# Query blocks eight ahead of the attention units instead of nine, the mixes on POOL by quarters, and the last residuals in another order

## What is computed

```python
xn = layernorm(x)                                   # (8, 100, 1024)
kv = concat([ctx, xn], axis=1)                      # (8, 461, 1024)
q = rms_norm((xn @ Wq) per head, q_norm_w)          # 32 heads of 128
k = rms_norm((kv @ Wk) per head, k_norm_w)          # 8 key heads
v = (kv @ Wv) per head
probs = softmax(q k^T / sqrt(128))                  # 4 query heads share one key head
x1 = x + tanh(g_xattn) * ((probs @ v) as rows @ Wo)
# then, on y = layernorm(x1):
logits = y @ router_w.T + router_b; two best of 8 experts, gates normalised
x2 = x1 + tanh(g_ffn) * sum over the two experts of gate * ((y @ A_e^T) @ B_e^T) * 0.5
```

## Time and profile before

| | |
|---|---|
| median of three runs | 1689.81 us |
| the profiled execution | 1685.8 us, of which the span of instructions is 1684.0 us |
| PE busy | 1650.3 us (98% of the span) |
| DVE, ACT, POOL busy | 1176.9, 877.3, 889.1 us |
| TensorE clock granted over the span | 0.998 of full speed |
| units and query blocks | about 684 to 1436 us |
| output product and tail | about 1321 to 1684 us |

### The profile page before, as it was taken

One profiled execution on the slowest core, in us unless ns is written; L12 is line 12 of the kernel. 1 busy time (PEld: TensorE's weight loads), 2 busy tenths in 40 slices (PEclk: granted clock), 3 DMA queues, 4 the chain that ended last, 5 costly groups with the idle time before them and its releaser, 6 DMA issues.

```text
span 1684.0 us, 26179 instructions
## 1 busy us (share of the span) xinstructions
PE 1650.3 (98%) x9120; PEld 1470.7 (87%) x9120; DVE 1176.9 (70%) x2054; ACT 877.3 (52%) x1663; POOL 889.1 (53%) x700
## 2 busy tenths in 40 slices
PE   7999999999999999999999999999999999999997
PEld 6788888678888879999999999999999889999995
DVE  7788886677777752677677777776766777556676
ACT  5545554544544431566666666666666666443432
POOL 1344443134434420777777777777776455563131
PEclk9999999999999999999999999999999999999999
DMA  5567778736566647556666666655556566687551
GB/s 200 157 171 235 232 207 249 194 112 188 151 180 164 159 161 235 173 166 208 197 213 198 198 204 189 191 190 180 182 171 205 187 215 218 229 281 248 222 178 58
DMA packets 238503, 323.87 MB, mean 192 GB/s; under 512 B 53300, under 2 KB 193396, under 8 KB 233380
## 3 DMA queue, kind: packets, MB, share of 16 engines
q1 hardware_dynamic: 237796, 315.65, 60.3%
q10 hardware_dynamic: 576, 6.55, 1.0%
HBM read 212.18 MB, written 109.97 MB: 191 GB/s over the span
## 4 chain that ended last, share of the span: by engine, by line
PE 89%; DVE 6%; ACT 3%; issue 2%; DMA 0%; POOL 0%; DVEq 0%; SPq 0%; ACTq 0%; POOLq 0%
PE bank L991 26%; PE bank L993 25%; PE bank L992 25%; PE bank L1129 5%; PE bank L1096 2%; PE bank L1025 1%; PE bank L1335 1%; DVE wo_lo L2024 1%; DVE mx L2004 1%; DVE at_lo L2026 1%; ACT pr L1611 1%; ACT w_hi L1427 1%; PE bank L1346 0%; DMA wr<-Wkv 0%; DVE pT_lo L1998 0%
## 5 line engine op out<-in xcount | busy, mean ns | idle before, releaser
L911 POOL TENSOR_SCALAR pr<-pr,rr 100x461 f32<-100x461 f32 x256 | 371.1, 1457 | 162.1 <-DVE rr L2019 162.1
L991 PE MATMUL bank<-w_hi,a_hi 128*128 128x512 f32 (+1 forms) x856 | 341.2, 399 | 11.0 <-DVE a_lo L1794 8.5
L993 PE MATMUL bank<-w_hi,a_lo 128*128 128x512 f32 (+1 forms) x856 | 335.2, 392 | 0.0
L992 PE MATMUL bank<-w_lo,a_hi 128*128 128x512 f32 (+1 forms) x856 | 334.3, 391 | 0.0
L1611 ACT ACTIVATE pr<-bank,nm,rq 100x461 f32<-100x461 f32 x256 | 188.7, 737 | 156.7 <-DVE nm L2010 155.0
L2004 DVE TENSOR_REDUCE mx<-bank 100x1 f32<-100x461 f32 x256 | 161.4, 631 | 78.5 <-PE bank L993 75.2
L865 POOL TENSOR_TENSOR msk<-ssk,epst 128x4 f32<-128x4 f32 (+1 forms) x60 | 22.9, 382 | 348.4 <-DVE ssk L1825 348.4
L991 PEld LDWEIGHTS bank<-w_hi,a_hi 128*128 128x128 f32 (+1 forms) x856 | 157.8, 184 | 48.4 <-issue 9.6
L993 PEld LDWEIGHTS bank<-w_hi,a_lo 128*128 128x128 f32 (+1 forms) x856 | 157.6, 184 | 38.4
L991 PE MATMUL bank<-xT_hi,wq_hi 128*128 128x400 f32 x512 | 188.3, 368 | 0.7 <-issue 0.7
L992 PEld LDWEIGHTS bank<-w_lo,a_hi 128*128 128x128 f32 (+1 forms) x856 | 158.0, 185 | 34.7
(11 more groups left out here) (159 smaller groups left out, 3556.1 us busy)
## 6 DMA issues: line engine op xcount, KB each, us to landing
kT_d<-kst SPq DMA_DIRECT2D x56, 512.0 KB, 5.6
v_d<-vst SPq DMA_DIRECT2D x56, 512.0 KB
kT<-kT_d SPq DMA_DIRECT2D x64, 361.0 KB, 4.5
kvr<-ctxT SPq DMA_DIRECT2D x44, 512.0 KB, 5.9
wq_raw<-Wq SPq DMA_DIRECT2D x32, 512.0 KB, 5.8
tb<-Wo SPq DMA_DIRECT2D x16, 1024.0 KB, 8.5
wt_d<-tb SPq DMA_DIRECT2D x16, 1024.0 KB, 7.8
wo_raw<-wt_d SPq DMA_DIRECT2D x16, 1024.0 KB, 7.4
```

The costliest lines, as they stand in the source:

```text
L911: pool.tensor_scalar(pr[0:NQ, u % 2, i], pr[0:NQ, u % 2, i], rr[0:NQ, i:i + 1], None, ALU.mult).then_inc(p_done, 1)
L991: pe.matmul(o, lh, rh, start=start, stop=False, skip_group_check=more)
L992: pe.matmul(o, lh, rl, start=False, stop=False, skip_group_check=more)
L993: return pe.matmul(o, ll, rh, start=False, stop=stop, skip_group_check=more)
```

## The change

`AHEAD` becomes 8, while the output product's parts still start in slot 56. So one block fewer is run before slot 0, slot u carries block u+8, and slot 55 is a full slot with block 63. `bare_slot` is gone; what it did for chunk 0 is spread out: its weights are split at the end of slots 53 and 54 (`first_weights`), its rows at the end of slot 55 (`first_heads`), and the square sums of block 63 move to slot 56. To make that possible the two buffers of `wo_hi`, `wo_lo`, `at_hi`, `at_lo` are laid out one by one. The loads of chunks 0 and 1 are issued in slots 51 and 53 instead of 53 and 54.

```diff
-AHEAD = 9
+AHEAD = 8
-OUT0 = LAST_Q
+OUT0 = LAST_Q - 1
+FIRST_W = {LAST_Q - 3: (0, 1), LAST_Q - 2: (2, 3)}
...
-            return ((4, 0), (5, 1), (4, 5), (0, 1))[t - TB][half] if t >= TB else 4 + half
+            return ((4, 0), (5, 1), (4, 0), (5, 1))[t - TB][half] if t >= TB else 4 + half
...
-                if u in (OUT0 - 2, OUT0 - 1):
-                    load_chunk(u - OUT0 + 2)
+                if u in (LAST_Q - 5, LAST_Q - 3):
+                    load_chunk((u - LAST_Q + 5) // 2)
...
             store(1)
             next_res(2)
+            next_res(3)
             store(2)
-            next_res(3)
```

On POOL the mixes are cut into four instructions each, and each group of four waits until DVE has split one more chunk:

```diff
             pool.wait_ge(oT_act, 6)
-            pool.tensor_tensor(oT_late[:, first], oT_late[:, first], oT_early[:, second], ALU.add).then_inc(mix_done, 1)
-            pool.tensor_tensor(oT_early[:, second], oT_early[:, second], oT_late[:, second], ALU.add).then_inc(mix_done, 1)
-            pool.wait_ge(mix_done, 2)
-            pool.tensor_tensor(oT_late[:, second], oT_late[:, second], oT_late[:, first], ALU.add).then_inc(mix_done, 1)
+            pool.wait_ge(wo_lo_done, split_after(FIRST_OF[P4] + 1))
+            for c in range(GQ):
+                pool.tensor_tensor(oT_late[:, c], oT_late[:, c], oT_early[:, GQ + c], ALU.add).then_inc(mix_done, 1)
+            pool.wait_ge(wo_lo_done, split_after(FIRST_OF[P4] + 2))
+            for c in range(GQ, C):
+                pool.tensor_tensor(oT_early[:, c], oT_early[:, c], oT_late[:, c], ALU.add).then_inc(mix_done, 1)
+            pool.wait_ge(wo_lo_done, split_after(FIRST_OF[P4] + 3))
+            pool.wait_ge(mix_done, 2 * GQ)
+            for c in range(GQ, C):
+                pool.tensor_tensor(oT_late[:, c], oT_late[:, c], oT_late[:, c - GQ], ALU.add).then_inc(mix_done, 1)
```

In `last_slot`, slot 56 gets the square of block 63 and what follows from it (here on PE; ACT and DVE have the like):

```diff
                 scores(u, 0)
+                if u == LAST_Q:
+                    squares(2 * H - 1)
                 turn_probs(u - 1, 0)
```

In the tail, PE turns the first halves of batches c and d ahead of the last chunk's end, a buffer of its own (`x1_last`) holds batch d's residual, and DVE takes the residuals in another order:

```diff
                 if n == 4 * GQ - 3:
                     turn_half(a, 0)
                     turn_half(b, 0)
+                if n == 4 * GQ - 2:
+                    turn_half(c, 0)
+                    turn_half(d, 0)
             last_half(0)
             last_half(1)
             low_rank(TB - 1)
-            turn_half(c, 0)
             last_half(2)
             last_half(3)
...
             low_rank(a)
-            turn_half(d, 0)
             turn_half(d, 1)
...
             residual_half(a, 0)
             residual_half(b, 0)
+            residual_half(c, 0)
+            residual_half(d, 0)
+            last_accumulators((0, 1))
             route_top(TB - 1)
-            residual_half(c, 0)
-            last_accumulators()
+            last_accumulators((2, 3))
+            residual_half(a, 1)
             route_gates(a - 1)
-            residual_half(a, 1)
             residual_half(b, 1)
             final(a - 1)
             residual_half(c, 1)
             route(a)
-            residual_half(d, 0)
             residual_half(d, 1)
```

More of the change, by code:

```diff
@@ L259, in build @@
         wo_raw = at("wo_raw", TMP, [P, 2, R, 512])
-        at_hi = at("at_hi", HI, [P, 2, TB, QW], F32R)
-        at_lo = at("at_lo", HI + 12800, [P, 2, TB, QW], F32R)
+        at_hi = [at(f"at_hi{k}", HI + 12800 * k, [P, TB, QW], F32R) for k in range(2)]
+        at_lo = [at(f"at_lo{k}", HI + 12800 * k + 6400, [P, TB, QW], F32R) for k in range(2)]
         oT_late = at("oT_late", HI + 25600, [P, C, TW])
         x1 = at("x1", HI + 38400, [P, 4, D])
+        x1_last = at("x1_last", RAW + 8 * KB, [P, D])
         at_raw = (at("at_raw0", RAW + 8 * KB, [P, TB, QW]), at("at_raw1", TMP + 16 * KB, [P, TB, QW]))
@@ L268, in build @@
         c_tmp = at("c_tmp", LO + 48640, [P, 2, TW])
-        wo_hi = at("wo_hi", WR, [P, 2, R, 512], F32R)
-        wo_lo = at("wo_lo", WR + 16 * KB, [P, 2, R, 512], F32R)
+        wo_hi = [at(f"wo_hi{k}", WR + 8 * KB * k, [P, R, 512], F32R) for k in range(2)]
+        wo_lo = [at(f"wo_lo{k}", WR + 8 * KB * (3 - k), [P, R, 512], F32R) for k in range(2)]
         oT = (oT_late, oT_early)
@@ L1255, in last_slot @@
                 values(u - 1, 3)
-            for u in range(OUT0):
+            for u in range(LAST_Q):
                 slot(u)
-            bare_slot(OUT0)
             for u in range(OUT0 + 1, UNITS):
@@ L1618, in keep_attn, with first_weights, first_heads @@
                 act.activation(ao[:, u % 2], ps[BPV][:, 0:QW], ACT.Copy).then_inc(ao_done, 1)
+            def first_weights(i):
+                if i == 0:
+                    act.wait_ge(wo_in[0], 16)
+                    act.wait_ge(wq_lo_done, H)
+                act.activation(wo_hi[0][:, i], wo_raw[:, 0, i], ACT.Copy).then_inc(wo_hi_done, 1)
+            def first_heads(i):
+                if i == 0:
+                    act.wait_ge(at_in[0], a_loaded(0))
+                    act.wait_ge(q_done, 2 * H - 1)
+                act.activation(at_hi[0][:, :, i * NQ:(i + 1) * NQ], at_raw[0][:, :, i * NQ:(i + 1) * NQ], ACT.Copy).then_inc(wo_hi_done, 1)
             def chunk_piece(m, i):
@@ L1642, in chunk_heads @@
                     act.wait_ge(at_in[m % 4], a_loaded(m))
-                act.activation(at_hi[:, m % 2], a_raw(m), ACT.Copy).then_inc(wo_hi_done, 1)
+                act.activation(at_hi[m % 2][:], a_raw(m), ACT.Copy).then_inc(wo_hi_done, 1)
             def accumulators(o):
@@ L2080, in slot @@
                     next_wq(n)
[L2082 to L2099 removed]
+                for i in FIRST_W.get(u, ()):
+                    first_weights(i)
+                if u == LAST_Q - 1:
+                    for i in range(R):
+                        first_heads(i)
             def last_slot(u):
@@ L2165, in residual_half, with last_accumulators @@
                     dve.bn_aggr(mv[0:NQ, t], bn6[0:NQ, t % 4]).then_inc(ag2_done, 1)
-            def last_accumulators():
-                dve.wait_ge(mix_done, 3)
-                for n in range(4):
+            def last_accumulators(some):
+                dve.wait_ge(mix_done, 3 * GQ)
+                for n in some:
                     dve.wait_ge(p3_done, n + 1)
```

140 lines of the change are left out of this document (53 added, 87 removed).

## The result

The changed kernel is slower: 1694.11 us in the median of 8 runs (1691.82 to 1699.03) against 1689.11 of the kernel before (1687.13 to 1690.82), a ratio of 1.0034 with a 95% interval of 1.0025 to 1.0043. Forecast were 1687.3, no change, and a range of 1684.3 to 1690.2, outside of which the result lies. The profiled execution took 1692.31, its span is 1690.5 against 1684.0.

A forecast was written before the change was run, and what follows sets the result against it. PE was taken to be busy nearly all of the span, so only its waits or low clock could be given back. Terms 0.2 − 1.2 − 2.45 + 0.9 = −2.55 took 1689.81 to 1687.3 us, range 1684.3 to 1690.2.

The forecast's parts named there:

- Full slots: Slots between 700 and 1307 us: PE has no waits, 11.35 us each, taken over unchanged; 0 from slot 1 to slot 53.
- Unit 0: Start of unit 0: `rq` holds `nm`, 2.1 us gained, 0.9 lost to half clock behind a PE gap; -1.2, ends -2.5 and +0.3.
- Rival (4): Slot 0 and tail: PE stays at half clock much longer behind the two new gaps; +4.3, 1694.1 us, chance 0.05.
- Slots 55 and 56: Slot 55 becomes full, slot 56 takes block 63's squares: 27.66 us against 27.41, +0.2, ends -0.5 and +1.0.
- Mixes: Block product P4: POOL's groups of four no longer delay DVE's splits, PE's waits go; -2.45, end -1.5.
- one of the prediction's own signs of being wrong: Sign for P4: the forecast is wrong if P4's waits come back.
- Tail: After the last product: later gates delay PE's `turn_h` and `up`; +0.9, ends -0.2 and +1.7.
- Faster and no change: Outcome chances for the whole kernel: faster, below 1686.4 us, 0.33; no change, up to 1693.2 us, 0.62.

The follow-up runs named there:

- sums_odd: Changed kernel with POOL's six extra weight sums behind slots 3, 5, 7, 43, 47 and 51 instead of 2, 4, 6, 42, 46 and 50; median 1691.36 us.
- before_odd: Kernel before with POOL's six extra weight sums moved behind slots 3, 5, 7, 43, 47 and 51; median 1697.11 us, ratio 1.0044.
- rms_first: Changed kernel with POOL's `rq` of unit 0 placed behind five of the eight weight sums instead of all eight; median 1691.98 us.
- tail_only: Kernel before with only the tail's order changed; median 1690.15 us, ratio 1.0001.
- after_loads: Changed kernel with the six loads spread: `ar` and `bm` behind P4's third and fourth chunks, one residual row behind each P2 chunk; 1690.48 us, ratio 1.0011.
- mix_spread: Kernel before with the mixes by quarters and the six loads spread over chunks of P4 and P2; 1684.68 us, ratio 0.9969.
- after: The changed kernel itself, with the whole change, against the kernel before; median 1694.11 us, ratio 1.0034.
- ahead_only: Changed kernel with mixes and tail put back, leaving query blocks eight ahead and new slots 53 to 56; median 1693.53 us, ratio 1.0022.
- all_fixes: Changed kernel with old tail, early `rq`, last three sums behind unit 0's scaling, extra sums behind odd slots, later chunk sums held, six loads in P2; ratio 1.0026.

## Why the prediction was wrong

**Full slots: the step that failed.** The prediction took "54 full slots in a row run at PE's own pace, 11.35 us each" over unchanged, and did not ask what moves against what when the blocks come one slot later. DVE's weight split changed parity against POOL's sums, and the stretch it had at nothing took +3.28. The trace of the kernel before held what was needed: `wq_lo` beside a sum was even used, for slot 0. In sums_odd the sums are moved and the six long slots are gone, though others grow because `rq` comes later; before_odd makes long slots in the other kernel by the same move, in part through `rq` too. The 0.4 of slot 11 are not explained.

**Unit 0.** The hold by `rq`, `nm` near 684 and the gap of nearly 4 us are as forecast; rms_first shows that this hold cost 5.1. The term missed its size (+0.13 for -1.2, within its ends) because the clock stayed low for 6.8 us instead of 3.3. sums_odd, with the same code there and 3.4 us of half clock, has slot 0 shorter by 1.5, which would make the term -1.4. Rival (4) named the longer low stretch for slot 0, with 0.05; its price of +2.4 was too high. That its total of 1694.1 is the measured median is luck: of its +4.3 it has +2.4 from slot 0, where +0.13 came, and +4.2 from the tail, where about +1 came with a low stretch of 3.4 us as forecast, and it has nothing for the slots.

**Behind the last slot.** The wait of 2.86 us comes from the same kind of contention, at a place whose instructions the change doesn't touch; it is chance as far as 14 profiles show, and in the changed kernel's only. Without the 2.45 us of that stretch the profile has +4.0.

**Slots 55 and 56.** Right: 27.62 for 27.66, a wait of 0.94 for the square.

**Mixes.** Right in that the splits go back to 1.82, wrong in "from here to the last product PE has no other wait that could take it up". The chunk's release also triggers the next load, which came to share the DMA engines with six others; -1.05 was left of -2.45 (tail order taken off by tail_only's 0.3). So P4's wait came back, one of the prediction's own signs of being wrong. after_loads and mix_spread show the cause, since spreading the loads takes the wait away in either kernel. The size of -2.45 was low as well: with no wait left it is 3.0.

**Tail.** Right: +0.75 in tail_only for +0.9.

**Chances.** Faster and no change had 0.95, and the median came out above the 1693.2 from which the prediction counts slower. The mean granted clock of the timed runs may account for some of what the terms above leave: 0.995 to 0.996 in the four kernels that keep the gap of 3.75 us (after, ahead_only, sums_odd, after_loads), 0.997 to 0.998 in those without a gap as long (all_fixes has another, of 5.51, and 0.995). Half clock for twice 0.002 of 1690 us is about 7 us more per run, an estimate of up to 3.4 us lost.

## What to carry to other kernels

When a stage is moved by one step of a loop, write down for each engine what stands beside it at every parity, above all what POOL does while DVE reads SBUF: a moved instruction meets others' work that was never moved. When a buffer comes free earlier, follow the transfer that this starts and what it will share the queue and the engines with; the mixes by quarters gained nothing here until six loads of 400 to 544 KB were spread. Look at the slack behind a meeting before charging it: one of 2.10 us was covered in 15 of 16 slots, one of 2.30 cost about 0.45 each time. And a gain that makes an engine wait for something else is worth only what the later clock leaves of it.

## What the runs showed of the hardware

- DVE and POOL held each other up in whole instructions: `wq_lo` took 1.23 alone, 2.30 beside a weight sum and 2.10 beside a sum of rows; `wo_lo` took 2.29 alone. Which gives way differed for the same two pieces of work: POOL's four sums 6.10 and DVE 2.73, or 4.06 and 5.33. The Trainium skill, "SBUF — State Buffer", section "SBUF: two separate sides", gives the port to whoever starts first, for the whole instruction. Most profiles agree; in the changed kernel's, DVE's split began during the first of the four sums and ended 2.2 us after the fourth, as if it had been passed over by the three between.
- Low stretches of the clock, added up over windows of 1 us, lasted 3.4 or 6.8 us. Behind the gap of 3.75 us at unit 0 one came in all four profiles that have it (6.8 three times, 3.4 once); behind waits of 0.95 to 2.04 us in slot 56 and in P4 in some only. Runs of one kernel differ by up to 11 us (sums_odd, 1688.80 to 1699.73), and its three longest have the lowest mean clock, 0.993 against 0.996 to 0.998; so one profile says little on a term of 1 us.
- Behind a listed wait of 0.73 or 1.73 us PE lost 0.89 and 2.00 in the chunk, 0.16 and 0.27 more than the list says (kernel before, against mix_spread).
